# Delta-rule attention on one core: VectorE's other work between its taps, a merge copy on ScalarE, the projection last in PE's slot

## What is computed

```python
q = l2norm(silu(conv4(x @ Wq))) * d ** -0.5        # 8 heads of 128
k = l2norm(silu(conv4(x @ Wk)))                    # 3 per token and head
v = silu(conv4(x @ Wv))                            # 3 per token and head
beta = 2 * sigmoid(x @ Wb); g = -exp(A_log) * softplus(x @ Wa + dt_bias)
def step(S, inp):                                  # over the 1024 tokens
    S = S * exp(gt)
    for i in range(3):
        S = S + bi * (ki * (vi - ki @ S))          # delta rule
    return S, qt @ S
x = layernorm(x + (rmsnorm(o) * silu(x @ Wg)) @ Wo)
x = layernorm(x + mixture_of_8_experts(x))         # not touched here
```

## Time and profile before

| | |
|---|---|
| runs | 8508.51 us median of 3 (8502.43 to 8517.87) |
| profiled execution, its own time | 8499.04 us |
| its span, first to last instruction | 8497.0 us |
| mean granted clock of TensorE | 0.956 of 2.4 GHz |
| PE, weight loads, VectorE, ScalarE, GpSimd busy | 89%, 75%, 78%, 62%, 48% of the span |
| one block in the steady part | 109 to 116 us |
| main loop | about 330 to 7480 us; the feed-forward part follows |

### The profile page before, as it was taken

One profiled execution on the slowest core, in us unless ns is written; L12 is line 12 of the kernel. 1 busy time (PEld: TensorE's weight loads), 2 busy tenths in 40 slices (PEclk: granted clock), 3 DMA queues, 4 the chain that ended last, 5 costly groups with the idle time before them and its releaser, 6 DMA issues. The chain is left out here.

```text
span 8497.0 us, 425999 instructions
## 1 busy us (share of the span) xinstructions
PE 7561.9 (89%) x155940; PEld 6383.7 (75%) x155940; DVE 6595.7 (78%) x22297; ACT 5290.1 (62%) x19575; POOL 4106.0 (48%) x6333
## 2 busy tenths in 40 slices
PE   5788988888889888888888889889898889979999
PEld 1677777777777777777777777777777777857777
DVE  3888888888888888888888888888888888733333
ACT  2566666666666666666666666666666666623333
POOL 0355555555555555555555555555555555511111
PEclk6799999999999999999999999999999999989999
DMA  2000000000000000000000000000000000010000
GB/s 86 5 9 9 9 10 9 9 9 9 10 9 10 9 9 9 9 10 9 10 10 9 10 9 9 10 8 10 9 9 9 10 9 10 8 29 10 7 10 8
DMA packets 283622, 97.66 MB, mean 11 GB/s; under 512 B 226096, under 2 KB 276544, under 8 KB 281152
## 3 DMA queue, kind: packets, MB, share of 16 engines
q1 hardware_dynamic: 281408, 68.93, 3.7%
HBM read 52.08 MB, written 16.78 MB: 8 GB/s over the span
## 5 line engine op out<-in xcount | busy, mean ns | idle before, releaser
L802 DVE SCALAR_TENSOR_TENSOR CY<-PP,CWV,CY 128x128 f32<-128x128 f32 x4608 | 1590.3, 345 | 102.2 <-ACT CY L721 1.4
L802 DVE SCALAR_TENSOR_TENSOR CY<-PP,CWK,CY 128x128 f32<-128x128 f32 x4608 | 1587.4, 344 | 83.9
L1004 POOL TENSOR_TENSOR UM<-U,C 32x256 f32<-32x256 f32 x1536 | 1104.8, 719 | 120.2 <-POOL UM L1004 20.8
L997 POOL TENSOR_TENSOR Y<-U,C 32x256 f32<-32x256 f32 x768 | 553.9, 721 | 1201.0 <-DVE UQ L880 1160.9
L516 PE MATMUL PP<-XT,WK 128*128 128x131 f32 x3072 | 741.5, 327 | 262.0 <-DVE CY L802 251.5
L516 PE MATMUL PP<-XT,WV 128*128 128x131 f32 x3072 | 756.6, 333 | 239.8 <-DVE CY L802 212.3
L977 POOL TENSOR_TENSOR S<-R,BETA 96x4 f32<-96x4 f32 x512 | 101.4, 198 | 1606.6 <-DVE R L840 1606.6
L536 PE MATMUL PI<-T,WB 32*32 32x32 f32 x49152 | 732.6, 194 | 138.7 <-DVE T L811 133.7
L536 PEld LDWEIGHTS PI<-T,WB 32*32 32x32 f32 x49152 | 623.2, 109 | 298.6 <-issue 230.2
L721 ACT ACTIVATE CY<-PP,CWK 128x128 f32<-128x128 f32 x1536 | 560.7, 365 | 453.8 <-PE PP L516 447.4
L820 DVE SCALAR_TENSOR_TENSOR S<-S,WHOLE,PK 128x128 f32<-128x128 f32 x2048 | 612.6, 341 | 253.1 <-PE PK L591 252.9
(11 more groups left out here) (228 smaller groups left out, 19080.8 us busy)
## 6 DMA issues: line engine op xcount, KB each, us to landing
EX<-exd SPq DMA_DIRECT2D x768, 32.0 KB, 2.2
exd<-EXS SPq DMA_DIRECT2D x16, 512.0 KB, 2.6
XR<-in_L_attn_x SPq DMA_DIRECT2D x65, 64.0 KB, 2.7
XL<-in_L_attn_x SPq DMA_DIRECT2D x16, 256.0 KB, 2.8
XRES<-in_L_attn_x SPq DMA_DIRECT2D x64, 64.0 KB, 3.0
x<-X SPq DMA_DIRECT2D x64, 64.0 KB, 1.6
XI<-x SPq DMA_DIRECT2D x16, 256.0 KB, 2.8
out<-OUT SPq DMA_DIRECT2D x16, 256.0 KB, 2.3
```

What stands on the lines that cost most here:

```text
L802: dve.scalar_tensor_tensor(CY[:, m % RING], ptile(m)[:, s:s + P], taps_of(m)[:, s:s + 1], CY[:, m % RING], ALU.mult, ALU.add).then_inc(tap ...
L997: pool.tensor_tensor(Y1[r, :, :], U[r, par, :, r], over(first[r, :], [BK, NHEAD, BK], 1), ALU.mult).then_inc(seed_sb, 1)
L1004: pool.tensor_tensor(UM[r, lv], U[r, par, :, r], over(merge[lv][r, :], [BK, NHEAD, BK], 1), ALU.mult).then_inc(made, 1)
```

## The change

- On PE, `project` moves from behind the inverse step to the end of the slot; `new_state` moves from slots 11 and 12 to 10 and 11.
- On ScalarE, the outputs of steps 2 and 6 of the inverse (the second Horner step of each level) are plain copies of the product into `T1`, where VectorE subtracted it from `base`. The third step becomes `T0 + W T1`, which is the same sum: I - W + W^2 - W^3. ScalarE's outputs stay ahead of its first tap, and the tap stays ahead of the slot's other work.
- On VectorE, the inverse outputs go from the slot's start behind tap 1, and the transposes behind tap 2. `add_state` of heads 4 to 7 is spread one head to a part over slots 0 and 1. Each reciprocal moves from part 0 to part 1, the sum `QSE` as well. `YL` moves to slot 13 of c = 2, its statistics and aggregate to slot 0 of c = 3, epsilon to slot 1, and `X1` from slot 1 to 4.
- On GpSimd, `RS` moves from the end of c = 2 into c = 3, behind the `YF` blocks.

```diff
--- before.py
+++ after.py
@@ -457,8 +457,8 @@
         def stage_bufs(k):
 
             base = (Y1, Y2)[k // 4]
-            return {"W0": (base, None, None), "W1": (base, None, None), "H": (base, base, T0), "H1": (base, T0, T1),
-                    "H2": (base, T1, (Y2, Y3)[k // 4])}[STAGES[k]]
+            return {"W0": (base, None, None), "W1": (base, None, None), "H": (base, base, T0), "H1": (None, T0, T1),
+                    "H2": (T0, T1, (Y2, Y3)[k // 4])}[STAGES[k]]
 
         def when(i, c):
 
@@ -624,8 +624,6 @@
                     for k in range(SLOTS):
                         if do_inv and k in INV_AT:
                             invert(invn, 1 - par, INV_AT[k])
-                        if known(i, 0, NSC):
-                            project(i, half, SLOTS * c + k)
                         if k in (1, 4) and do_run:
                             old_state(k // 4, run, rs, rc)
                         if k in (1, 3) and do_prep:
@@ -657,8 +655,8 @@
                             solve(k - 8, run, prep, do_prep)
                         if k == 11 and do_run:
                             read_out(run, rc)
-                        if k in (11, 12) and do_run:
-                            new_state(k - 11, run, rc, prep, do_prep)
+                        if k in (10, 11) and do_run:
+                            new_state(k - 10, run, rc, prep, do_prep)
                         if k in (12, 13) and do_prep:
                             rows_v(k - 12, c, sc, prep, run, do_run)
                         if k in (8, 10) and out_now:
@@ -697,6 +695,8 @@
                             if gate_now:
                                 pe.wait_ge(gsil_sb, 2 * i)
                             transpose_x(i + 1, 1 - half)
+                        if known(i, 0, NSC):
+                            project(i, half, SLOTS * c + k)
 
                 pe.wait_ge(ready, READY)
                 transpose_x(0, 0)
@@ -710,9 +710,10 @@
                     out_now = c == 2 and known(i - 2, 0, NSC)
                     gate_now = c == 3 and known(i - 1, 0, NSC)
                     for k in range(SLOTS):
-                        if do_inv and k in INV_AT and INV_AT[k] in (0, 4):
+                        if do_inv and k in INV_AT and INV_AT[k] in (0, 2, 4, 6):
                             act.wait_ge(inv_ps, STEPS * invn + INV_AT[k] + 1)
-                            act.activation(WB[:, :, :], inv, ACT.Copy).then_inc(inv_sb, 1)
+                            to = WB if INV_AT[k] in (0, 4) else T1
+                            act.activation(to[:, :, :], inv, ACT.Copy).then_inc(inv_sb, 1)
                         if known(i, 0, NSC):
                             m = SLOTS * c + k
                             T = TILES * i + m
@@ -808,37 +809,52 @@
                     if k == 7:
                         need(dve, diag_sb, NBK * w)
                         need(dve, join_ps, 3 * w - 1)
-                    dve.tensor_tensor(to[:, :, :], base[:, :, :], inv, ALU.subtract).then_inc(inv_sb, 1)
+                    dve.tensor_tensor(to[:, :, :], base[:, :, :], inv, ALU.subtract if STAGES[k] == "H" else ALU.add).then_inc(inv_sb, 1)
 
                 def flip(to, of):
                     return dve.transpose(to[:, :, :].rearrange("p h c -> p (h c)"), of[:, :, :].rearrange("p h c -> p (h c)"))
 
-                def add_state(l, run, part):
+                def add_state(l, run, part, parts):
                     if part == 0:
                         dve.wait_ge(s_ps, 2 * run + l + 1)
-                    for h in heads[l][2 * part:2 * part + 2]:
+                    for h in heads[l][LH // parts * part:LH // parts * (part + 1)]:
                         op = dve.scalar_tensor_tensor(S[:, h], S[:, h], WHOLE[:, run, h:h + 1], PK[:, h], ALU.mult, ALU.add)
-                    if part == 1:
+                    if part == parts - 1:
                         op.then_inc(s_sb, 1)
 
                 def group(i, half, c, k, part):
 
                     ahead, prep, invn, run, do_ahead, do_prep, do_inv, do_run = when(i, c)
+                    norm_now = c == 3 and known(i - 2, 0, NSC)
                     rc, par = (c - 2) % 4, c % 2
                     out_now = c == 2 and known(i - 2, 0, NSC)
                     gate_now = c == 3 and known(i - 1, 0, NSC)
                     next_x = c == 3 and known(i + 1, 1, NSC)
-                    if k == 0 and known(run - 1, 0, NCH):
-                        add_state(1, run - 1, part)
+                    if do_inv and k in INV_AT and INV_AT[k] not in (0, 2, 4, 6) and part == 0:
+                        inv_out(invn, INV_AT[k])
+                    if do_inv and INV_AT.get(k) == 3 and part == 1:
+                        dve.wait_ge(inv_sb, STEPS * invn + 4)
+                        flip(XB, Y2).then_inc(x2t_sb, 1)
+                    if do_inv and INV_AT.get(k) == 7 and part == 1:
+                        dve.wait_ge(inv_sb, STEPS * invn + 8)
+                        need(dve, join_ps, 3 * (invn - 1) + 1)
+                        for b in range(2):
+                            r = slice(BK * b, BK * b + BK)
+                            op = dve.transpose(X3[r, :, r], Y3[r, :, :])
+                        op.then_inc(x3t_sb, 1)
+                    if k in (0, 1) and known(run - 1, 0, NCH):
+                        add_state(1, run - 1, 2 * k + part, 4)
                     if k in (3, 5) and do_prep and part == 0:
                         l = k // 5
                         dve.wait_ge(ssr_sb, 2 * prep + l + 1)
                         need(dve, rt_sb, prep)
                         dve.tensor_scalar(SSE[:, lanes[l]], SSR[:, c, lanes[l]], EPS_L2, None, ALU.add).then_inc(sse_sb, 1)
+                    if k in (3, 5) and do_prep and part == 1:
+                        l = k // 5
                         dve.wait_ge(sse_sb, 2 * prep + l + 1)
                         need(dve, kds_sb, 2 * prep - 1 + l)
                         dve.reciprocal(R2[0:R, lanes[l]], SSE[0:R, lanes[l]]).then_inc(r2_sb, 1)
-                    if k == 10 and c == 3 and do_prep and part == 0:
+                    if k == 10 and c == 3 and do_prep and part == 1:
                         dve.wait_ge(ssr_sb, 2 * prep + 2)
                         for j in range(LH):
                             op = dve.tensor_scalar(QSE[CT * j:CT * j + CT], SSR[R:P, :, j:NHEAD:LH], EPS_L2, None, ALU.add)
@@ -879,20 +895,23 @@
                         else:
                             dve.tensor_tensor(UQ[0:R, c, lanes[l]], PK[0:R, lanes[l], R:P], EM[0:R, lanes[l], R:P], ALU.mult).then_inc(u_sb, 1)
                     if k == 11 and do_run:
-                        add_state(0, run, part)
-                    if k == 12 and out_now and part == 0:
+                        add_state(0, run, part, 2)
+                    if k == 13 and out_now and part == 1:
                         q = i - 2
                         dve.wait_ge(wo_ps, q + 1)
                         dve.wait_ge(xres_in[half], 8 * (q + 2 - half) if not isinstance(q, int) else 16 * ((q + 2) // 2))
                         dve.tensor_tensor(YL[:, :], PB[:, 0:P], XRES[:, half], ALU.add).then_inc(y_sb, 1)
-                        dve.wait_ge(y_sb, q + 1)
+                    if k == 0 and norm_now and part == 0:
+                        dve.wait_ge(y_sb, i - 1)
                         dve.bn_stats(ST[:, :], YL[:, :]).then_inc(st_sb, 1)
-                        dve.wait_ge(st_sb, q + 1)
+                    if k == 0 and norm_now and part == 1:
+                        dve.wait_ge(st_sb, i - 1)
                         dve.memset(spare[:, :], 0.0)
                         dve.bn_aggr(MV[:, :], ST[:, :]).then_inc(mv_sb, 1)
-                        dve.wait_ge(mv_sb, 2 * q + 1)
+                    if k == 1 and norm_now and part == 0:
+                        dve.wait_ge(mv_sb, 2 * (i - 2) + 1)
                         dve.tensor_scalar(MV[:, 1:2], MV[:, 1:2], EPS_LN, None, ALU.add).then_inc(mv_sb, 1)
-                    if k == 1 and c == 3 and known(i - 2, 0, NSC) and part == 0:
+                    if k == 4 and norm_now and part == 1:
                         q = i - 2
                         dve.wait_ge(rs_sb, q + 1)
                         need(dve, x1_out[half], 8 * (q - half) if not isinstance(q, int) else 16 * (q // 2))
@@ -909,18 +928,6 @@
                     gate_now = c == 3 and known(i - 1, 0, NSC)
                     next_x = c == 3 and known(i + 1, 1, NSC)
                     for k in range(SLOTS):
-                        if do_inv and k in INV_AT and INV_AT[k] not in (0, 4):
-                            inv_out(invn, INV_AT[k])
-                            if INV_AT[k] == 3:
-                                dve.wait_ge(inv_sb, STEPS * invn + 4)
-                                flip(XB, Y2).then_inc(x2t_sb, 1)
-                            if INV_AT[k] == 7:
-                                dve.wait_ge(inv_sb, STEPS * invn + 8)
```

(13 more changed lines are left out.)

## The result

| | before | changed |
|---|---|---|
| median of the runs | 8505.47 us (4 runs) | 9013.47 us (4 runs) |
| all runs | 8498.15 to 8517.87 | 8997.63 to 9022.28 |
| profiled execution, its own time and span | 8499.04, 8497.0 | 9022.28, 9020.2 |

The ratio is 1.0593, with a 95% interval of 1.0575 to 1.0611: 508 us slower, 7.9 us in each of the 64 blocks. I had forecast slower by 0.4%, and the time lies far above the range.

The account below looks back on a forecast made before the run. VectorE was taken to bound step 7 to step 2 of the inverse, PE the rest. Legs of -3.2 and +3.2 us a block cancel; 0.5 us added over 64 blocks gives 8540 us, range 8365 to 8700.

Parts of the forecast that it names:

- R2: Rival: longer single PE stops bring the low clock into the PE-bound leg; +192 us, 8730 us; chance 0.16.
- second legs: Inverse step 2 to the next step 7, set by PE; new stops make 73.6 us a block against 70.4.
- first legs: Inverse step 7 to the next inverse's step 2, set by VectorE; 35.9 us a block against 39.1.
- the two legs cancel: Over one block of 109.5 us, 3.2 us less in one leg and 3.2 us more in the other: 0.0 us.
- (1): Second leg, new_state in slot 10: PE waits for ScalarE's BZ, 0.45 us a chunk, 1.8 a block.
- (3): Second leg, fifth inverse step in slot 8: PE waits for VectorE's flip, 0.5 us, 1.05 in c = 2; 2.6 a block.
- (2): Second leg, rows_v in slot 12: PE waits for OSB, 0.25 us each, 0.9 a block.
- R1: Rival: first leg's gain stays, second leg's stops are covered; 8304 us in full, 8370 to 8400 at half; chance 0.31.
- R3: Rival: the scheme is neutral, the legs cancel and the added 0.5 us a block isn't there; 8508 us; chance 0.05.

Follow-up runs that it names:

- run 5: Changed kernel with idle matmuls cut to each chunk's stop (2, 6, 10, 7 behind slot 3's projection, four more in c = 0): 8595.77 us, ratio 1.0112.
- run 9: Changed kernel with projection back behind the inverse step and 1, 4, 8, 4 idle matmuls, but without ScalarE's two copies (back on VectorE): 8245.94 us against 8236.3.
- run 11: Kernel of run 6 with VectorE's inverse outputs and transposes back ahead of tap 1 of their slot: 8334.96 us, ratio 0.9807.
- run 12: Kernel of run 6 with new_state back in slots 11 and 12: 8283.1 us, ratio 0.9745.
- run 1: Changed kernel with PE's projection back behind the inverse step, all else of the change kept: 8429.7 us, ratio 0.9885.
- run 7: Changed kernel with five idle matmuls behind the projection of slot 9, where PE has no stop: 9321.97 us, ratio 1.0963.
- run 6: Changed kernel with the projection back behind the inverse step and 1, 4, 8, 4 idle matmuls behind rows_k of slot 3: 8236.3 us, ratio 0.9686.
- run 13: Changed kernel with two idle matmuls behind the projection of slot 3 in every chunk: 8754.61 us, ratio 1.0273.

## Why the prediction was wrong

**The step that failed is the price and the chance of R2.** Its mechanism is what happened. It was given 0.16 and 3 us a block, "if one low stretch of 6 us more per block follows". In the block shown, three low stretches hold 27 us, and 8.4 us of the second legs are theirs (81.7 against 73.3 at full clock). The price of a single stretch was not too low: 6.8 us of low clock cost 2.15 us in c = 1 (18.91 against 16.76), a third and not a half. Their number was. Three inputs failed. The longest stops were put at 2.4 (c = 2) and 1.6 (c = 3); they are 2.8 and 2.0, and 1.57 in c = 1, where I had 0.9. PE's wait for SiLU in c = 0, 0.35 before, was in no term; it is 1.29, and c = 0 has a low stretch in 11 of 15 blocks. And I took the frequency from a handful of stops in the kernel before. Its trace held the answer, had I counted all of them: of 48 stops of 1.00 to 1.24 us none is followed by a low stretch, of 40 of 1.25 to 1.74 us 11 are, and of the 7 longer ones, which lie in the leg behind the loop edge, all (counted as in the last section). By my own forecast of one stop of 2.4 us a block, a low stretch in nearly every block was likely, and it was priced as unlikely. The low clock also costs less where VectorE is the bound: in the kernel before, first legs of c = 3 with 3.4 us of low clock took 10.5 to 10.8 us, those without 10.2 to 10.5. Before, the second legs held 1.3 us of low clock a block on average, now 27.

**The second legs were right at full clock, the first legs in part.** Second legs: 73.6 forecast, 73.3 in run 5. First legs: 35.9 forecast, 37.0 measured, so the gain is 2.1 us a block and not 3.2; the difference is mostly c = 0, where PE waits for SiLU, 9.72 against 8.75. Behind the loop edge, once in two blocks, the first leg of c = 0 is no shorter but 1.2 us longer (14.5 against 13.3 on average), which was in no term either. For the block shown, "the two legs cancel" would nearly hold at full clock: 37.1 + 73.3 = 110.4 against 109.5 before, and 8596 us in run 5 against my 8540. (1) The stop for BZ: 0.45 forecast, 0.40 measured, 66 times in 66 chunks. (2) The stop for OSB: 0.25 forecast, about 0.2. (3) The late flip in slot 8: there, and largest in c = 2 as said (1.12 in run 5, 1.05 forecast), but a stop of 0.3 for KD ahead of the Gram product, which wasn't in the sum, takes part of it.

**The copies on ScalarE**, costed at nothing for ScalarE and 0.66 us a chunk for VectorE, are worth 10 us in all (run 9). **The order between taps** is worth 0.39 us a chunk (run 11). **new_state** was held to be off the chain; it is worth 0.7 us a block (run 12). R1 did not arise: its stops stayed. R3's 8508 isn't reached even with the clock held (8596, run 5).

What stays open: why one stop of 1.6 or 2.0 us is followed by a low stretch and the next of the same length isn't. The stop of 1.97 in c = 3 of the block shown passed without one. Length alone doesn't order them: in the changed kernel all 8 stops of c = 1 of 1.55 to 1.58 us are followed by one, and only 1 of the 7 of 1.71 to 1.72.

## What to carry to other kernels

Cost a new order in two currencies: the sum of PE's idle time, and the length of each single stop, weighed by how often stops of that length are followed by a low clock in the trace of before, and look for the waits that the new order lengthens in every part of the loop, not only in the one you follow. Two short stops that become one long one can cost more than their sum, if what follows is bound by PE. Where the profile's granted clock falls behind a stop, putting matmuls into the stop tells whether the stop is the cause: on this kernel some 7 us of idle matmuls a block (29 of 0.23) bought back 418 of 508 us, and the better cure was an order that splits the stop (run 1), with both together at 8236.

## What the runs showed of the hardware

More matmuls made the kernel faster: 285 us less with five idle ones in front of the stop, 309 us more with the same five elsewhere. The granted clock of 3000 to 5000 us is here in three kernels, the one before, run 7 and run 6:

```profile
3000.00:5000.00 2000.00, 1791.03 (x41875) 1559.05 (x41875) 1722.72 (x5826) 1358.00 (x5286) 1112.32 (x1750) 0.97 0.05 9
```

```profile
3000.00:5000.00 2000.00, 1828.59 (x38148) 1619.95 (x38149) 1495.53 (x5084) 1251.31 (x4859) 997.25 (x1568) 0.86 0.04 8
```

```profile
3000.00:5000.00 2000.00, 1884.19 (x44215) 1658.02 (x44213) 1723.88 (x5909) 1461.79 (x5653) 1165.09 (x1825) 0.98 0.05 10
```

0.97, 0.86 and 0.98, with PE busy for 1791, 1829 and 1884 us: the kernel with the low clock has more busy time than the first. I counted PE's stops of 1.0 us and more for VectorE's taps or outputs from 3000 to 4800 us, and took the mean granted clock of the 6 us that begin 0.5 us after each. "Low" are those with a mean under 0.9; the entries are low of all.

```
stop, us            1.00-1.24   1.25-1.74   1.75-2.24   2.25 and more
before                 0/48       11/40        1/1           6/6
changed                 -          9/15       12/18         19/19
two idle (run 13)      1/16        9/18        3/4          15/15
projection back (1)    3/33         -          8/8          15/16
```

Four kernels agree: next to nothing up to 1.24 us, between a quarter and two thirds of the stops around 1.5, most around 2, all but one beyond. In the last column 6, 7, 6 and 8 are stops of 2.4 to 3.4 us behind the loop edge. Two idle matmuls take the stops of c = 1 from 9 of 15 to 1 of 16.

The table leaves out the stops for SiLU in c = 0, and they don't fit it: of 15 in the changed kernel, 1.24 to 1.29 us long, 11 are followed by a low stretch; with two idle matmuls behind them the stops are as long, but only 3 of 15 are. So what stands around a stop counts too; how, is not shown. Of the 5.1 us a block by which the second legs of run 13 are shorter, 2.4 are in c = 0 and 1.5 in c = 1.

At the low level a row of the profile shows it at once, 1.07 us for an inverse step of 0.70 and 0.80 for a projection of 0.49. The Trainium skill (TensorE: Matmul & The Clock Gate, "HAM oscillation — how this bites in real kernels") describes how the clock falls behind waits for DMA transfers that return in every turn of a loop, and advises to order the loop so that fewer of them stand between the matmuls. Run 1 agrees: by order alone the clock rises from 0.884 to 0.934. The waits told of there are longer ones for transfers; here 1.2 to 2.8 us for VectorE and ScalarE were enough.
